# Attention's first layer on the tensor engine, two tiles at a time

## The reference

```python
x = x + _L0_xattn_ref(_layernorm(x), ctx_1024, ctx_1024, mask, Wq, Wk, Wv, Wo)   # layer one
x = x + _L0_attn_ref(_layernorm(x), Wq, Wk, Wv, Wo, W_down_kv, W_up_k, W_up_v)   # layer two
x = x + _L0_ffn_ref(_layernorm(x), w1, b1, w2, b2)                               # FFN, rounded to 8 bits
```

```python
scores = jnp.einsum('bhqd,bhkd->bhqk', Q, K) / np.sqrt(D_KEY)
scores = jnp.where(mask[:, None, None, :] == 0, NEG_INF, scores)
scores = jnp.where(causal[None, None, :, :], NEG_INF, scores)
attn = jax.nn.softmax(scores, axis=-1)
out = jnp.einsum('bhqk,bhkd->bhqd', attn, V)
return out.transpose(0, 2, 1, 3).reshape(B, Nq, D_MODEL) @ Wo
```

## Time and profile before

| | |
|---|---|
| median of 3 runs | 315.71 us (314.49 to 316.68) |
| the profiled execution | 315.6 us, of which its span is 313.7 us |
| PE busy | 288.6 us, 92% of the span |
| DVE busy | 255.1 us, 81% |
| ACT busy | 239.8 us, 76% |
| POOL busy | 232.2 us, 74% |

### The profile page before, as it was taken

One profiled execution on the slowest core, in us unless ns is written; L12 is line 12 of the kernel. 1 busy time (PEld: TensorE's weight loads), 2 busy tenths in 40 slices (PEclk: granted clock), 3 DMA queues, 4 the chain that ended last, 5 costly groups with the idle time before them and its releaser, 6 DMA issues. The chain is left out here.

```text
span 313.7 us, 13645 instructions
## 1 busy us (share of the span) xinstructions
PE 288.6 (92%) x5744; PEld 198.1 (63%) x5744; DVE 255.1 (81%) x555; ACT 239.8 (76%) x529; POOL 232.2 (74%) x183
## 2 busy tenths in 40 slices
PE   7769979999999999999999999999999999699583
PEld 2347647676767767685768686867777777332273
DVE  2887779999888888887888787878788998579864
ACT  3584958585869898787888888898878877699580
POOL 5686849766888978799999999999899952430230
PEclk9998999999999999999999999999999999899869
DMA  7999000000000000000000000000000000000027
GB/s 232 309 276 288 9 2 4 2 2 5 4 2 2 4 2 3 5 2 2 4 2 5 3 4 2 5 3 5 2 2 4 2 5 5 0 0 2 0 67 203
DMA packets 16542, 11.64 MB, mean 37 GB/s; under 512 B 5153, under 2 KB 14690, under 8 KB 16482
## 3 DMA queue, kind: packets, MB, share of 16 engines
q1 hardware_dynamic: 15762, 10.34, 12.0%
q10 hardware_dynamic: 720, 0.43, 0.5%
HBM read 8.67 MB, written 2.10 MB: 34 GB/s over the span
## 5 line engine op out<-in xcount | busy, mean ns | idle before, releaser
L843 ACT ACTIVATE pt<-ps 128x512 f32<-128x512 f32 x128 | 75.9, 594 | 21.4 <-PE ps L591 20.6
L411 POOL TENSOR_TENSOR u<-u,mx 128x1024 f32<-128x1024 f32 x32 | 60.8, 1903 | 26.8 <-DVE mx L1059 26.6
L403 POOL TENSOR_TENSOR ud<-u,con 128x1024 f32<-128x1024 f32 x31 | 73.5, 2371 | 1.5 <-DVE u L1045 1.4
L1040 DVE SCALAR_TENSOR_TENSOR u<-ps,rs,arena 128x1024 f32<-128x1024 f32 x32 | 40.9, 1279 | 15.0 <-PE ps L572 13.3
L572 PE MATMUL ps<-arena,qT 32*64 32x256 f32 x1024 | 44.3, 402 | 6.4 <-ACT arena L836 4.0
L1045 DVE TENSOR_SCALAR u<-ps 128x1024 f32<-128x1024 f32 x32 | 39.0, 1219 | 12.5 <-PE ps L572 12.1
L618 PE MATMUL ps<-pt,vx 128*32 128x64 f32 x2048 | 41.4, 222 | 1.8 <-DVE oT L981 0.9
L618 PEld LDWEIGHTS ps<-pt,vx 128*32 128x32 f32 x2048 | 32.5, 111 | 15.5 <-issue 9.3
L624 PE MATMUL ps<-pt,con 128*32 128x128 f32 x1024 | 40.0, 275 | 0.0
L1059 DVE TENSOR_REDUCE mx<-u 128x16 f32<-128x1024 f32 x32 | 38.7, 1210 | 0.1
L572 PEld LDWEIGHTS ps<-arena,qT 32*64 32x64 f32 x1024 | 14.9, 129 | 32.7 <-issue 21.6
(11 more groups left out here) (153 smaller groups left out, 550.7 us busy)
## 6 DMA issues: line engine op xcount, KB each, us to landing
out<-pt SPq DMA_DIRECT2D x8, 256.0 KB, 3.0
arena<-in_ctx_cols SPq DMA_DIRECT2D x4, 256.0 KB, 4.5
xn3T<-in_x_cols SPq DMA_DIRECT2D x4, 256.0 KB, 4.7
x<-in_x SPq DMA_DIRECT2D x4, 256.0 KB, 5.2
arena<-in_ctx_cols SPq DMA_DIRECT2D x2, 512.0 KB, 5.8
xn3T<-in_x_cols SPq DMA_DIRECT2D x2, 512.0 KB, 5.3
x<-in_x SPq DMA_DIRECT2D x2, 512.0 KB, 8.6
arena<-in_mask_BxS_if SPq DMA_DIRECT2D x2, 256.0 KB, 6.7
```

What stands on the lines that cost most here:

```text
L403: pool.tensor_tensor(dh, uh, decay.unsqueeze(1).to_broadcast([P, H, HALF]), ALU.mult)\
L411: pool.tensor_tensor(uh, uh, mx[:, n % 4, 0:count].unsqueeze(2).to_broadcast([P, count, HALF]), ALU.subtract)\
L843: act.activation(pt[:, n % 2, 4 * half:4 * half + 4].rearrange("p h n -> p (h n)"), ps[:, bank, :], ACT.Exp).then_inc(s["emptied"], 1)
L1040: dve.scalar_tensor_tensor(by_head(u[:, n % UB]), sc, rs[:, 0, n:n + 1], mask[:, n].unsqueeze(1).to_broadcast([P, H, HALF]), ALU.mult, ALU ...
```

## The change

In layer one TensorE takes tiles in pairs, in every second turn. In an even turn n it does the scores of tiles n and n+1, then values and sums of tiles n-4 and n-3; in an odd turn n neither, but at the end of it, after the pieces, the projections of tiles n-5 and n-4 into one bank. Transposes stay one tile per turn. The scores of the odd tile go to the columns that the even one leaves free in banks 0 to 3; values and sums of the odd tile go to the other half of bank 7 (`SUMS`). VectorE reads both tiles' scores at the start of the even turn, once both are done; maxima stay one per turn. Logarithm, exponential of minus, division and addition to `x` are done for two tiles in one instruction of 256 columns. `UB` goes from 3 to 4. Layer two keeps its order; its odd tiles use the other half of bank 7 too, and tile 63 now waits for the division of tile 62.

```diff
@@ -30,7 +30,7 @@
-UB = 3
+UB = 4
@@ -57,7 +57,7 @@
-LAG_T, LAG_SHIFT, LAG_PV, LAG_ADD = 2, 3, (3, 4), (4, 5)
+LAG_T, LAG_SHIFT, LAG_PV, LAG_ADD = 2, 3, 4, 5
@@ -88,9 +88,14 @@
-def due(turn, lags):
-    return [n for n, of_layer in ((turn - lags[0], range(NT)), (turn - lags[1], range(NT, NS))) if n in of_layer]
+def pair_at(turn, lag):
+    return [n for n in [turn - lag] if n in range(0, NT, 2)]
+def single_at(turn, lag):
+    return [n for n in [turn - lag] if n in range(NT, NS)]
@@ -112,7 +117,7 @@
-        order += [("o", n) for n in due(turn, LAG_ADD)] + keys + pieces[turn]
+        order += [("o", n) for n in single_at(turn, LAG_ADD)] + keys + pieces[turn] + [("o", n) for n in pair_at(turn, LAG_ADD)]
@@ -452,7 +455,7 @@
-                        pe.wait_ge(s["x_added"], before[1] + 1)
+                        pe.wait_ge(s["x_added"], before[1] + (2 if before[1] < NT else 1))
@@ -561,15 +564,16 @@
-                if 1 <= n <= NT:
+                if 2 <= n <= NT and n % 2 == 0:
 ...
+                half = slice(HALF * (n % 2), HALF * (n % 2) + HALF) if layer == 0 else slice(0, HALF)
 ...
-                        last = pe.matmul(ps[HALF * b:HALF * (b + 1), r].rearrange("p (h k) -> p h k", h=HR)[:, :, 0:HALF],
+                        last = pe.matmul(ps[HALF * b:HALF * (b + 1), r].rearrange("p (h k) -> p h k", h=HR)[:, :, half],
@@ -607,32 +611,35 @@
-                j, i, bank = n // GT, t % GT, num_den(n)
+                j, i, first = n // GT, t % GT, 2 * P * (n % 2)
 ...
-                if 1 <= n < NS - 1:
+                if n >= 1 and (layer or n % 2 == 0):
 ...
-                            pe.matmul(ps[32 * r:32 * (r + 1), bank, HALF * b:HALF * (b + 1)],
+                            pe.matmul(ps[32 * r:32 * (r + 1), OB, first + HALF * b:first + HALF * (b + 1)],
 ...
-                        last = pe.matmul(ps[32 * r:32 * (r + 1), bank, P:2 * P], ones[:, par],
+                        last = pe.matmul(ps[32 * r:32 * (r + 1), OB, first + P:first + 2 * P], ones[:, par],
 ...
-                pe.wait_ge(s["o_ready"], n + 1)
+                tiles = (n,) if layer else (n, n + 1)
+                pe.wait_ge(s["o_ready"], tiles[-1] + 1)
 ...
-                pe.matmul(ps[:, bank, 0:D], oT[:, n % 2], wo[:, layer], start=True, stop=True)\
-                    .then_inc(s["wo_done"], 1)
+                for tile in tiles:
+                    pe.matmul(ps[:, bank, (tile - n) * D:(tile - n + 1) * D], oT[:, tile % 2], wo[:, layer],
+                              start=True, stop=True).then_inc(s["wo_done"], 1)
@@ -653,28 +660,36 @@
-                if n < NS:
+                if n < NT and n % 2 == 0:
+                    scores(n)
+                    scores(n + 1)
+                if NT <= n < NS:
 ...
-                for tile in due(n, LAG_PV):
+                for tile in pair_at(n, LAG_PV):
 ...
-                for tile in due(n, LAG_ADD):
+                    values(tile + 1)
+                for tile in single_at(n, LAG_PV):
+                    values(tile)
+                for tile in single_at(n, LAG_ADD):
 ...
-                if n == NS + LAG_ADD[1]:
+                if n == NS + LAG_ADD:
 ...
+                for tile in pair_at(n, LAG_ADD):
+                    project(tile)
@@ -843,15 +858,17 @@
-            def log_den(n):
-                act.wait_ge(s["pv_done"], n + 1)
-                act.activation(lden[:, n % 2], ps[:, num_den(n), P:2 * P], ACT.Ln).then_inc(s["ln_done"], 1)
-            def inv_den(n):
-                act.wait_ge(s["ln_done"], n + 1)
+            def log_den(n, count):
+                act.wait_ge(s["pv_done"], n + count)
+                e = slice(n % 2, n % 2 + count)
+                act.activation(lden[:, e], SUMS[:, e, 1], ACT.Ln).then_inc(s["ln_done"], count)
+            def inv_den(n, count):
+                act.wait_ge(s["ln_done"], n + count)
 ...
-                    act.wait_ge(s["o_ready"], n - 1)
-                act.activation(rden[:, n % 2], lden[:, n % 2], ACT.Exp, scale=-1.0).then_inc(s["den_ready"], 1)
+                    act.wait_ge(s["o_ready"], n - 2 + count)
+                e = slice(n % 2, n % 2 + count)
+                act.activation(rden[:, e], lden[:, e], ACT.Exp, scale=-1.0).then_inc(s["den_ready"], count)
@@ -879,12 +896,15 @@
-                for tile in due(n, LAG_PV):
-                    log_den(tile)
+                for tile in pair_at(n, LAG_PV):
+                    log_den(tile, 2)
+                    inv_den(tile, 2)
+                for tile in single_at(n, LAG_PV):
+                    log_den(tile, 1)
 ...
-                for tile in due(n, LAG_PV):
-                    inv_den(tile)
+                for tile in single_at(n, LAG_PV):
+                    inv_den(tile, 1)
@@ -969,17 +989,18 @@
-            def add_residual(n):
-                layer, t = layer_of(n)
-                dve.wait_ge(s["wo_done"], n + 1)
-                dve.tensor_tensor(x[:, t], ps[:, RB + slot["o", n] % NR, 0:D], x[:, t], ALU.add).then_inc(s["x_added"], 1)
-            def divide(n):
-                dve.wait_ge(s["den_ready"], n + 1)
+            def add_residual(n, count):
+                t = n % NT
+                dve.wait_ge(s["wo_done"], n + count)
+                dve.tensor_tensor(x[:, t:t + count], ps[:, RB + slot["o", n] % NR, 0:count * D].rearrange("p (t d) -> p t d", d=D),
+                                  x[:, t:t + count], ALU.add).then_inc(s["x_added"], count)
+            def divide(n, count):
+                dve.wait_ge(s["den_ready"], n + count)
 ...
-                    dve.wait_ge(s["wo_done"], n - 1)
-                dve.tensor_tensor(oT[:, n % 2], ps[:, num_den(n), 0:P], rden[:, n % 2], ALU.mult)\
-                    .then_inc(s["o_ready"], 1)
+                    dve.wait_ge(s["wo_done"], n - 2 + count)
+                e = slice(n % 2, n % 2 + count)
+                dve.tensor_tensor(oT[:, e], SUMS[:, e, 0], rden[:, e], ALU.mult).then_inc(s["o_ready"], count)
@@ -1014,6 +1035,23 @@
+            def scores_of(e):
+                every = ps[:, 0:RG, :].rearrange("p g n -> p (g n)").rearrange("p (h k) -> p h k", h=H)
+                return every[:, :, HALF * e:HALF * (e + 1)]
+            def read_scores(n):
+                if n >= UB:
+                    dve.wait_ge(s["filled"], fill["t", n - UB, 1] + 1)
+                for m, (_, t0, _, _) in enumerate(MAKE):
+                    if n == t0:
+                        dve.wait_ge(s["mask_ready"], m + 1)
+                dve.wait_ge(RS[0], batch_of(0, n))
+                dve.wait_ge(s["s_done"], 2 * (n // 2) + 2)
+                dve.scalar_tensor_tensor(by_head(u[:, n % UB]), scores_of(n % 2), rs[:, 0, n:n + 1],
+                                         mask[:, n].unsqueeze(1).to_broadcast([P, H, HALF]),
+                                         ALU.mult, ALU.add).then_inc(s["s_read"], 1)
@@ -1025,27 +1063,19 @@
-                sc = ps[:, 0:RG, :].rearrange("p g n -> p (g n)").rearrange("p (h k) -> p h k", h=H)[:, :, 0:HALF]
 ...
-                if UB <= n < NT + UB:
-                    dve.wait_ge(s["filled"], fill["t", n - UB, 1] + 1)
-                elif NT + UB <= n < NS:
-                    dve.wait_ge(s["decayed"], n - NT - UB + 1)
-                if n < NT:
-                    for m, (_, t0, _, _) in enumerate(MAKE):
-                        if n == t0:
-                            dve.wait_ge(s["mask_ready"], m + 1)
-                    dve.wait_ge(RS[0], batch_of(0, n))
+                for tile in (n, n + 1) if n < NT and n % 2 == 0 else ():
+                    read_scores(tile)
+                if NT <= n < NS:
+                    if n < NT + UB:
+                        dve.wait_ge(s["filled"], fill["t", n - UB, 1] + 1)
+                    else:
+                        dve.wait_ge(s["decayed"], n - NT - UB + 1)
 ...
-                    dve.scalar_tensor_tensor(by_head(u[:, n % UB]), sc, rs[:, 0, n:n + 1],
-                                             mask[:, n].unsqueeze(1).to_broadcast([P, H, HALF]),
-                                             ALU.mult, ALU.add).then_inc(s["s_read"], 1)
-                elif n < NS:
-                    dve.wait_ge(s["s_done"], n + 1)
-                    dve.tensor_scalar(by_head(u[:, n % UB]), sc, CLAMP, -CLAMP, ALU.min, ALU.max)\
+                    dve.tensor_scalar(by_head(u[:, n % UB]), scores_of(0), CLAMP, -CLAMP, ALU.min, ALU.max)\
 ...
-                for tile in due(n, LAG_ADD):
-                    add_residual(tile)
+                for tile in single_at(n, LAG_ADD):
+                    add_residual(tile, 1)
@@ -1058,28 +1088,32 @@
-                for tile in due(n, LAG_PV):
+                for tile in pair_at(n, LAG_ADD):
+                    add_residual(tile, 2)
+                for tile in pair_at(n, LAG_PV):
+                    divide(tile, 2)
+                for tile in single_at(n, LAG_PV):
 ...
-                        divide(tile)
+                        divide(tile, 1)
 ...
```

(8 more changed lines are left out.)

5 lines of the change are left out of this document (2 added, 3 removed).

## The result

The changed kernel takes **321.31 us** (median of 4 runs, 320.79 to 322.52) beside 315.28 of the kernel before on the same chip: ratio 1.0195, 95% interval 1.0158 to 1.0233. It is 6.0 us slower, where 3.8 us less was forecast, and outside the range. The profiled execution took 321.42 us, its span 319.4. Ratios and intervals here are of runs in the usual state; a few runs of the kernel before, at about 319 us, were in a slower one and are left out of them.

What follows compares the result with a forecast made beforehand. TensorE was taken to bound the kernel, busy 74.84 of 75.50 us from turn 12 to 32, with DVE also full in turns 10 to 16. Terms -0.5 + 1.3 + 3.0 = 3.8 us took 315.6 to 311.8; range 308.5 to 317.

Steps and rivals of the forecast that it cites:

- The switching: TensorE's time lost where the shape of array parts changes: 1.04 us a pair before, 0.53 after, 0.51 saved.
- rival 2: On TensorE a pair's second scores cost 0.62 us, weight loads exposed; 313.6 us in all, chance 0.08.
- Wide instructions on DVE and ACT: Two tiles per instruction: DVE's division 0.42 us instead of 0.56, 0.29 saved per pair with the residual; ACT 0.4, off path.
- POOL's queue at turn 8: A later first maximum delays POOL's mask and tile 9's subtraction; scores of turn 12 come at 57.8 against 57.34.
- The last tile's wait: In layer two the last tile's values wait for tile 62's division, at most 0.9 us, narrowly covered by POOL's norms.
- The slower pace of 7.2 us: In turns 12 to 17 DVE's own work sets 7.2 us per pair in place of 7.63; 1.3 us gained.
- the ring: Projections wait for a bank ACT must empty: 0.3 us every second pair, up to 0.9 at turn 22, 0.6 in all.
- the start: Up to turn 12 the edit loses 0.5 us, turn 8's scores still at 42.5; bounds: gain 1.5, loss 1.5.
- layer two and the rest: Layer two keeps its order and was to take as long as before; no term in the sum.
- bunching: Ring banks, ACT and DVE wait for things coming two at a time, 0.3 to 0.4 a pair; 315.0 us, chance 0.23.
- Rival 4: The odd tile's subtraction on POOL becomes the pace, each of 12 pairs losing 0.3 us; 319.2 us, chance 0.14.
- theory I: From the follow-up expectations: in a long run of small matmuls TensorE's instructions come late; no size or chance given.

Runs made afterwards that it cites:

- proj_in_7: Changed kernel, but a pair's projections go to the left half of bank 7 and the next values wait for the addition to x; 316.88 us, ratio 1.0046.
- reads_split: Changed kernel with TensorE's order untouched, but VectorE reads one tile's scores a turn, the odd tile's in the odd turn; 321.80 us, ratio 1.0168.
- values_only: Changed kernel with scores and their reads one tile a turn again, values, sums, divisions, projections and additions still in pairs; 316.49 us, ratio 1.0043.
- late_pairs: Changed kernel with scores and reads one tile a turn up to tile 11 and in pairs from tile 12 on; 317.18 us, ratio 1.0048.
- narrow_after: Changed kernel with logarithm and exponential of the sums on 16 columns of each tile instead of 128; 318.44 us, ratio 1.0113.
- values_mask_tail: Kernel with values in pairs and scores single, plus the last mask made in turn 9 and tile 63's values in bank 3; 316.59 us, ratio 1.0034.
- pairs_from_4: Changed kernel with the scores of tiles 0 to 3 each in its own turn, pairs from tile 4 on; 318.85 us, ratio 1.0089.
- values_first: Changed kernel with a pair's values and sums ahead of its scores from turn 4 on, and the division ahead of VectorE's reads; 320.05 us, ratio 1.0144.
- proj_mask_tail: Changed kernel with a pair's projections in bank 7, the last mask made in turn 9 and tile 63's values in bank 3; 316.85 us, ratio 1.0028.
- late_pairs_7: Changed kernel with scores in pairs only from turn 12, projections in bank 7 and tile 63's values in bank 3; 315.10 us, ratio 0.9982.
- scores_only: Kernel before with only layer one's scores and their reads in pairs and 4 buffers of u, values, divisions and projections single; 333.14 us, ratio 1.0581.

## Why the prediction was wrong

**What held.** The switching: second scores cost 0.43, not 0.62, so rival 2 is refuted. The 16 weight loads of the second tile, 0.13 us each, would be 2.1 us in a row. The Trainium skill (TensorE: Matmul & The Clock Gate, section Part 3: Packing small matmuls) lets a weight load overlap matmuls in flight only where the row groups differ. The trace does not agree: the 32 loads of the values use all the rows and still stand in a step of 0.47 us. A pair that waits for nothing takes 7.49 - 0.33 - 0.07 = 7.09 us, against 7.1 forecast, and 7.15 to 7.16 in proj_in_7. Wide instructions on DVE and ACT cost 0.41 and 0.39 to 0.42, as taken. POOL's queue at turn 8 was forecast to take 15.3 us from the scores of turn 8 to those of turn 12 and took 15.41, with the wait of the transposes for POOL where it was put; reads_split, where the first maximum comes earlier, took 14.49. The last tile's wait was covered: POOL's seven norms are one block again, 5.54 us. The slower pace of 7.2 us that DVE was to set in turns 12 to 17 is not seen: the pairs of turns 14 and 16 take 7.49 and 7.50 like those behind them.

**The step that failed: the ring.** "I take 0.6 in all." The mechanism was named, with its bank, its engine and its size, 0.3 in each pair that begins at a turn 4j+2, "and up to 0.9 at turn 22". The five pairs with a piece of queries wait 0.33 us each and start their scores another 0.07 late: 2.0 us. Even the forecast's own numbers gave 1.5 for these alone, and it wrote 0.6: a slip of the sum. The other pairs were taken to be free, and are not. In those of turns 20 and 28 the projections come 0.27 and the scores behind them another 0.07 late, 0.7 in both; the second piece waits 0.55 and 0.88, behind the transposes at 101.8 and 109.8, for ACT's copies, which stand behind weights that ACT prepares; transposes wait 0.3 at 94.7. Against the forecast of 71.15 us from turn 12 to 32 the trace has 78.51. Of these 7.4 us the waits for the ring and for ACT are about 4.4, and the three pauses in the middle of values 2.4. The other 0.6 is spread over steps next to weights' preparations, of which I have no account. Moving the projections out of the ring took 4.71 us away: 2.3 of the waits and the 2.4 of the pauses, while the waits at 101.8 and 109.8 stayed. So the forecast's term of 0.6 was 4.4 us of waits, and a loss of 2.4 us for which it had no term stood beside it.

**The second: the start.** "The scores still start at 42.5, since ACT's expansion releases them" did not hold: they came at 43.42, 0.94 later, and this with the forecast's 0.5 behind it makes the 1.49. The prediction's own bound had it, "a loss of 1.5 if ACT's expansions slip behind a later exponential". At turn 4 ScalarE shows that order, in the kernel after:

```profile
21.82 1.08 ACT L858 ACTIVATE pt<-ps 128x512 f32<-128x512 f32 x2
22.79 0.81 ACT L851 ACTIVATE arena<-kT,cst,con 128x512 f32<-128x512 f32 x1
```

and in the kernel before, where the exponential comes earlier:

```profile
21.48 0.60 ACT L843 ACTIVATE pt<-ps 128x512 f32<-128x512 f32 x1
21.96 0.82 ACT L836 ACTIVATE arena<-kT,cst,con 128x512 f32<-128x512 f32 x1
```

The scores of turn 4 follow the expansion, 23.65 against 22.83. That values in pairs gain 2.4 us up to turn 12 by themselves (values_only, at the same granted clock of 0.84 from 20 to 31 us) was not seen at all; pairs of scores give it back and more.

**The third: layer two and the rest, taken at nothing.** 0.60 from turn 32 to tile 63 in the changed kernel, and 0.35 to 0.97 in every run that has the values of layer one in pairs with values behind scores. It lies where the last pairs of layer one meet layer two's single tiles: 0.61 of it is there at the scores of tile 33, and behind tile 37 nothing is added. Of the 0.55 behind tile 63 I can only say that this stretch ran from 59.94 us at a clock of 0.93 to 62.40 at 0.84 over the kernels, most of which have the same work in it.

Of the rivals, bunching named the right mechanism and gave it 315.0 and at most 317. It was sized per pair, 0.3 to 0.4; the waits and pauses came to 0.7. It also named a spell at half clock behind the new pause in front of tile 9's transposes: that pause, 1.17 us, was followed by 1.00, but the spell ahead of turn 8 was longer than before (0.69 against 0.84 from 20 to 31 us). Rival 4 came nearest in time, 319.2, for a reason that is not there.

**What stays open.** What the pauses are. I counted TensorE's entries, matmuls and weight loads together, up to each pause. In the changed kernel they stand behind 1729, 3009 and 4289 entries, 1280 apart. In late_pairs, reads_split, narrow_after and values_mask_tail there are pauses behind the same three numbers, in pairs_from_4, values_only and values_first behind 3009 and 4289; in values_first these entries are scores, in values_only sums. So a pause is bound to a place in the order of instructions and not to a step or a bank, which speaks for a late supply (theory I) and does not show it. It is not always there: with the projections in bank 7, proj_in_7 and proj_mask_tail have none and late_pairs_7 only the first, though TensorE's order is nearly the same, and the kernel before and scores_only have none. What decides it, no run shows. Nor is it known whether the change lowers the clock. And values_only, ahead of the kernel before by 1.8 us at turn 32 in its trace, is 0.9 us behind in the medians: its profiled execution, 315.17 us, was the quickest of its ten.

## What to carry over

When work is put in pairs, price the consumer that now sits idle for half the pair and then gets everything at once: its busy time falls, and its last result, which frees the producer's buffers, comes later. Sum such a wait over every pair in which it stands, and give the ones without a number their own row, before calling a mechanism "0.6 in all". A pair's output that closes a loop belongs in a buffer that is free by then anyway, not in a ring behind the slowest reader. And compare traces only where their clocks are alike, or say how much of the difference lies where they are not.

## What the runs showed of the hardware

The second of two tiles' 32x64 matmuls cost 0.43 us after the first's 0.62, switch included, with 16 more weight loads on the same rows. A 256-column division or addition took 0.41 to 0.42 us where one of 128 took 0.28. Clocks: in values_first TensorE was busy for 0.67 us between 50 and 54 us, and from 54 to 58 its granted clock was 0.58, half clock for most of it (1.2 of 2.4 GHz); in the changed kernel the waits of 1.32 us at turn 8 and 1.17 in turn 11 were followed by 1.00. TensorE's pauses without a releaser, in the middle of a step, were 0.35 to 0.95 us of idle time in most cases, 30.4 to 32.2 us apart, and stood behind the same counts of its entries in nine of the kernels with values in pairs.
